# Attention inside a three-part transformer kernel: matmul steps regrouped in threes, and the rotary multiply by the sine moved ahead of the pair swap

## What is computed

```
x = x + 0.5 * ffn(layernorm(x))
x = x + attn(layernorm(x))
x = x + 0.5 * ffn(layernorm(x))

attn(x):                                  # 16 heads of 64
    h = layernorm(x) * ln_scale + ln_bias
    c_q, c_kv = h @ w_down_q.T, h @ w_down_kv.T           # 256 -> 128
    q, k, v = c_q @ w_up_q.T, c_kv @ w_up_k.T, c_kv @ w_up_v.T
    q, k = rope(q), rope(k)      # rot = (e*cos - o*sin, e*sin + o*cos), e and o the even and odd dims
    out = softmax(q @ k.T / 8) @ v
    return out @ w_out.T + x
```

## Time and profile before

| | before |
|---|---|
| time, median of 3 runs | 4203.93 us (4203.29 to 4210.23) |
| time of the profiled execution | 4204.82 us |
| its span, first to last instruction | 4202.9 us |
| PE busy, share of the span | 3943.4 us, 94% |
| DVE, ACT, POOL busy | 2964.9, 2769.4, 3018.6 us (71%, 66%, 72%) |
| mean granted TensorE clock | 0.986 |

### The profile page before, as it was taken

One profiled execution on the slowest core, in us unless ns is written; L12 is line 12 of the kernel. 1 busy time (PEld: TensorE's weight loads), 2 busy tenths in 40 slices (PEclk: granted clock), 3 DMA queues, 4 the chain that ended last, 5 costly groups with the idle time before them and its releaser, 6 DMA issues. The chain is left out here.

```text
span 4202.9 us, 66226 instructions
## 1 busy us (share of the span) xinstructions
PE 3943.4 (94%) x24908; PEld 2235.9 (53%) x24908; DVE 2964.9 (71%) x3709; ACT 2769.4 (66%) x3532; POOL 3018.6 (72%) x1634
## 2 busy tenths in 40 slices
PE   7999979999999999999999999999999999989999
PEld 6888834444444444444444444444444444468888
DVE  5656568777777776877777777777777877555563
ACT  4444457777777777777777777777776777744544
POOL 3444458888888887888788788888887888734443
PEclk9999989999999999999999999999999999999999
DMA  3333221112211211121122112111211121133331
GB/s 110 106 121 112 73 91 54 57 54 67 71 52 52 79 54 52 60 78 51 52 65 69 53 56 81 52 51 59 74 55 57 58 72 62 42 110 105 121 111 61
DMA packets 192775, 300.39 MB, mean 71 GB/s; under 512 B 50327, under 2 KB 100936, under 8 KB 191816
## 3 DMA queue, kind: packets, MB, share of 16 engines
q1 hardware_dynamic: 192456, 296.17, 21.9%
HBM read 201.20 MB, written 26.73 MB: 54 GB/s over the span
## 5 line engine op out<-in xcount | busy, mean ns | idle before, releaser
L1072 DVE TENSOR_REDUCE atNM<-atPS 128x2 f32<-128x1024 f32 x1024 | 1208.0, 1220 | 568.5 <-PE atPS L873 563.0
L1170 POOL TENSOR_TENSOR atACC<-atACC,atPT 128x1024 f32<-128x1024 f32 x510 | 1277.2, 2504 | 69.0 <-ACT atPT L1010 15.0
L1010 ACT ACTIVATE atPT<-atPS 128x1024 f32<-128x1024 f32 x1024 | 995.3, 1022 | 197.3 <-PE atPS L894 187.3
L905 PE MATMUL atPO<-atPT,atV 128*64 128x512 f32 x4096 | 972.5, 595 | 0.0
L1001 ACT ACTIVATE atPS<-atSH 128x1024 f32<-128x1024 f32 x768 | 767.5, 1023 | 39.7 <-DMA atSH<-atMD 24.9
L1170 POOL TENSOR_TENSOR atACC<-atPT 128x1024 f32<-128x1024 f32 x255 | 624.7, 2450 | 105.7 <-PE atOT L927 102.8
L873 PE MATMUL atPS<-atKH,atQH 64*128 64x512 f32 x2048 | 456.5, 448 | 124.0 <-ACT atPT L1010 112.3
L1149 POOL TENSOR_TENSOR atVT<-atVT,atSIN 128x512 f32<-128x512 f32 x254 | 331.0, 1303 | 295.9 <-DMA atVT<-atR 295.9
L905 PEld LDWEIGHTS atPO<-atPT,atV 128*64 128x64 f32 x4096 | 281.6, 137 | 472.9 <-issue 466.6
L894 PE MATMUL atPS<-atQH,atKL 64*128 64x512 f32 x2048 | 469.0, 454 | 38.0 <-ACT atPS L1001 35.2
L894 PE MATMUL atPS<-atQH,atKH 64*128 64x512 f32 x2048 | 405.3, 391 | 0.0
(11 more groups left out here) (280 smaller groups left out, 6835.9 us busy)
## 6 DMA issues: line engine op xcount, KB each, us to landing
atSH<-atMD SPq DMA_DIRECT2D x128, 512.0 KB, 4.5
atVT<-atR SPq DMA_DIRECT2D x508, 128.0 KB, 2.1
f1GB<-f1GD SPq DMA_DIRECT2D x128, 256.0 KB, 7.2
f2GB<-f2GD SPq DMA_DIRECT2D x128, 256.0 KB, 6.9
atRSUM<-atRD SPq DMA_DIRECT2D x126, 256.0 KB, 4.0
X<-x SPq DMA_DIRECT2D x4, 1024.0 KB, 6.0
XS<-x SPq DMA_DIRECT2D x16, 256.0 KB, 3.9
x<-X SPq DMA_DIRECT2D x16, 256.0 KB, 2.7
```

Source lines behind the costliest of these rows:

```text
L905: ins = pe.eng.matmul(PO[HI[h], :], V[n % 2][:, j, HI[h]], PT[k % NPT][:, h, :], start=j == 0, stop=j == T - 1)
L1010: act.eng.activation(PT[k % NPT][:, :, :], PS[ring.of[step]][:, :, :], ACT.Exp, scale=SCALE).then_inc(grown.sem)
L1072: dve.eng.tensor_reduce(NM[:, q // 4, :, q % 4, t], PS[ring.of[step]][:, :, :], AX.X, ALU.max, negate=True).then_inc(most_out.sem)
L1170: pool.eng.tensor_tensor(total[:, :, :], begun[:, :, :], PT[k % NPT][:, :, :], ALU.add).then_inc(gathered.sem)
```

## The change

- The tables' keys become ticks, one for each tile, 16 a unit (`begin` and `early` the even ticks, `late` and `end` the odd).
- The order is written three tiles at a time (`x`, `x + 1`, `x + 2`), as two groups of three uses of the ring: score, most, score, and then most, score, most. One fill stands between the two exponentials of the first group. The attend of tile `x - 1` and the others of tick `x` follow the first group, the attends of `x` and `x + 1` and the others of `x + 1` and `x + 2` the second.
- `sine` and its multiply on POOL go, and ACT's copy of the piece to `R`. DVE multiplies the piece by the sine into `R` straight from `OT`, ahead of the swap, and by the cosine as before. `rotate` moves from DVE to POOL, and subtracts where it added, since the swap now turns the sign.
- `high` of k moves one tick ahead, `high` of q to where that of k stood, `shift` one tick ahead. `NAT` goes from 3 to 4.

```diff
-    NAT = 3
+    NAT = 4
...
-            begin, early, late, end = {}, {}, {}, {}
+            begin, early, late, end = ((0, 0), {}), ((0, 1), {}), ((1, 0), {}), ((1, 1), {})
...
-                table.setdefault(PER * (m - 1) + period, []).extend(steps)
+                (tick, _), steps_of = table
+                steps_of.setdefault(2 * (PER * (m - 1) + period) + tick, []).extend(steps)
...
                     at(early, m, k - 6, ("raise", m, i, t))
-                    at(end, m, k - 5, ("sine", m, i, t))
-                    at(late, m, k - 4, ("rotate", m, i, t))
-                at(early, m, 0, ("high", m, 1))
-                at(end, m, 0, ("high", m, 0), ("klow", m))
+                    at(end, m, k - 5, ("rotate", m, i, t))
+                at(end, m, -1, ("high", m, 1))
+                at(early, m, 0, ("high", m, 0))
+                at(end, m, 0, ("klow", m))
...
-                    at(end, m, 6 + 4 * t, ("shift", m, t))
+                    at(early, m, 6 + 4 * t, ("shift", m, t))
...
+            for x in range(-42, 2 * PER * (NN + 4), 3):
+                order += tile("score", x) + most_of(x) + tile("fill", x + 2) + tile("score", x + 1)
+                order += others_of(x) + tile("attend", x - 1)
+                order += [step for step in tile("gather", x - 1) if step[3] % 4 and step[1:3] + (step[3] // 4,) != (NN - 1, 1, 1)]
+                order += most_of(x + 1) + tile("score", x + 2) + most_of(x + 2)
+                if x % T == T - 1:
+                    order += tile("fill", x + 3) + tile("attend", x) + others_of(x + 1) + tile("fill", x + 4) + tile("attend", x + 1)
+                else:
+                    order += tile("fill", x + 3) + others_of(x + 1) + tile("fill", x + 4) + tile("attend", x) + tile("attend", x + 1)
+                order += [step for i in range(2) for step in tile("gather", x + i)
+                          if step[3] % 4 and step[1:3] + (step[3] // 4,) != (NN - 1, 1, 1)] + others_of(x + 2)
...
@@ scalar
-                    elif name == "raise":
...
-                        act.eng.activation(R[k][:, :], place(step), ACT.Copy).then_inc(raw.sem)
@@ vector, raise
-                        dve.wait_ge(*raw(n, i, t))
+                        dve.wait_ge(*raised(n, i, t))
...
+                        dve.eng.tensor_tensor(R[k][:, :], place(step), SIN[:, sl], ALU.mult).then_inc(raw.sem)
...
-                    elif name == "rotate":
...
-                        dve.eng.tensor_tensor(U[:, i, sl], U[:, i, sl], VT[k][:, :], ALU.add).then_inc(rotated.sem)
@@ gpsimd
-                    elif name == "sine":
+                    elif name == "rotate":
...
-                        pool.eng.tensor_tensor(VT[k][:, :], VT[k][:, :], SIN[:, t * 512:(t + 1) * 512], ALU.mult).then_inc(sined.sem)
+                        pool.wait_ge(*cosine(n, i, t))
+                        pool.eng.tensor_tensor(U[:, i, sl], U[:, i, sl], VT[k][:, :], ALU.subtract).then_inc(rotated.sem)
```

38 lines of the change are left out of this document (14 added, 24 removed).

## The result

| | before | after |
|---|---|---|
| time, median of 4 runs each on one chip | 4206.96 us (4203.29 to 4210.23) | 4152.01 us (4144.14 to 4158.46) |
| ratio, 95% interval | | 0.9869 (0.9849 to 0.9889) |
| profiled execution | 4204.82 us | 4144.14 us |

The change saves 55 us, 1.3%. The sign is the forecast's and the time lies in its range of 3980 to 4200, but the gain is less than half of the 116 us forecast, and the time is 2 us above the 4030 to 4150 that the forecast gave its own chance of 0.61: it falls at the edge of rival 2's stretch. The profiled execution of the changed kernel is the fastest of its four, so the two traces differ by 61 us where the medians differ by 55.

A forecast was written before the change was run, and what follows sets the result against it. PE, busy 94% of the span, was taken as the bound. -184 + 68 = -116 us, with 144 us of new waits and 118 of old taken as equal: 4204.8 - 116 = 4089 us. Range 3980 to 4200; 4030 to 4150 at 0.61.

The forecast's parts named there:

- rival 2: POOL becomes attention's bound, its waits staying whole: 47.8 us a unit, about 4169 us; chance 0.10 (4150 to 4213).
- The wait of the second most: On PE, the second most waits 0.36 us for an exponential in each of 512 periods; threes remove it: 184 us saved.
- The crossings: On PE, 171 more ways there and back between 64-row and 128-row steps, at 0.4 us each: 68 us added.
- The new waits: New order's stalls: empty middle slot 45, raise in second slot 43, end of head's half 30, shift 26; together 144 us.
- the old ones: Score weight loads' 241 waits for ACT's fill before the change, less 0.23 us hidden each: 118 us, replaced by the new order.
- The rotation at 0: Rotation moved among POOL, DVE and ACT: 178 us less DVE work, but none is the bound, so 0 from the path.
- the bound of 25 us: DMAs and queues, SP's hold of swaps included: priced at 0, at most one engine crossing, 0.1 us x 254.
- The shift: Its row stands 8 us ahead of its fill; ACT 0.6 us over in 43 of 128 halves: 26 us, bounds 0 and 205.
- Rival 1: PE nears its own bound, new waits hiding behind each other and old fill waits gone: 3971 us; chance 0.19 (3940 to 4030).
- Rival 3: Fill between two exponentials, late DVE: PE stalls 0.7 us in each of 341 triples, 239 us, 4328 us; chance 0.10 (above 4213).
- Rival 4: The 0.59 us between two mosts is a property of mosts, no wait for the ring; given no chance of its own.
- The signs: Expected in trace: most's waits below 100 us, unit 46.5 us, maxima 1.22 us, score waits for fills below 174, `atSH` 25 to 100.

The follow-up runs named there:

- split_mosts: The kernel before with one line changed: early steps (a raise or a value) put between the two mosts; 4163.48 us.
- extra_crossing: The changed kernel with the attend of the tile before moved between the first score and first most of each triple; 4482.46 us.
- rotate_dve_four: The changed kernel with the rotation's subtract on DVE, at the tick of the old add, and four buffers VT instead of two; 4200.08 us.
- threes_alone_four: The new order in threes with the rotation of before, and four buffers VT instead of two; 4327.1 us.
- both_light: The changed kernel with each maximum over half the keys and each fill over half the columns (work left out); 4009.13 us.
- pool_light: The changed kernel with POOL's rotation and division over only 128 of each 512 columns (work left out); 4151.37 us.
- fill_behind: The changed kernel with the fill between the two exponentials of a triple put behind both; 4146.14 us.
- middle_fill_dve: The changed kernel with DVE making the middle fill of each triple, 341 fills instead of 256; 4140.29 us.
- middle_shift: middle_fill_dve with the shift's read put right behind its write on SP, one tick earlier; 4144.39 us.
- most_first: The changed kernel with each triple's first group as most, score, score: 4145.18 us; a second version with DVE's fills reassigned to match: 4144.76 us.
- no_branch: The changed kernel without the branch where a head's half ends, so a fill stands ahead of the attends there too; 4182.2 us.
- threes_alone: The new order in threes with the rotation of before (ACT's copy, sine on POOL, add on DVE); 4376.56 us.
- rotation_alone: The order of before with the new rotation (sine multiply on DVE, subtract on POOL, no ACT copy); 4254.61 us.

## Why the prediction was half right

**The wait of the second most, -184: right.** PE's delays there were 188 us, the mosts never stand side by side, and split_mosts saves 42 us by this alone, net of some 155 us of crossings.

**The crossings, +68: right in kind, a little too dear.** 0.35 us each by the rows of after and of extra_crossing, where 0.4 was taken; that is 60 us for 171. With all delays under 0.15 us the rise is 43 us. Part of the difference: the first 128-row step followed a second most after 0.43 us and follows a score or a lone most after 0.32, so the 0.20 read at that place was half a crossing and half the late start of the second most. The late starts that went with the wait gave back some 30 us; the forecast had taken their 0.10 us for a part of the crossings' price. The condition "wrong if the crossings cost more than 0.4" was not met.

**The new waits, 144, against the old ones, 118: the step that failed.** The text said "Against them stand the old waits for fills, 118 us, which this order replaces ... I take these two as equal." The new side came out about as sized. With the 62 us of delays that were no waits for fills before (12 at attends, 50 into `OT`) it makes 206, and PE's delays after are 197. Its split was off: scores and mosts 98, attends 39, `OT` 60. The old side was the error. It was taken from 241 waits of the weight load, 174.1 us, less 0.23 us each. PE itself stood idle for those fills far less, as another row of the same view of before shows:

```profile
PE atPS L894 <- ACT atPS L1001: 35.2, 47, 4.9
```

The same row of the changed kernel has 35.2 us too, in 77 times, so this row shows the size of the error but not the change; the starts show both.

On PE's starts all delays of scores and mosts before, other than the second most's, are 51 us. Of the 174.1 us, 128.7 (128 waits) passed beside attends, whose pairs run for 0.43 us and more, and 36.1 (109 waits) beside scores. With 51 in the place of 118 the same sum gives -184 + 68 + 144 - 51 = -23, and with the 43 measured for crossings and small delays in the place of 68, -48; the units measured -57.5. That the two remaining errors are small is in part luck: the new side's parts were off by up to 30 us each, with both signs. The starts would have shown this ahead of time, as they did for the most.

**The rotation at 0: wrong as a part, and not seen as a partner.** Alone it costs 47 us and the order in threes alone 168 (up to 58 of it by the clock); only together do they gain. Two terms hid in the zero. The two multiplies hold `OT` (the forecast had them, at 43 us, but only for the raise in the second slot; in the order of before they cost 49). And SP: "SP, which holds a swap until the one before is rotated, is held for less. I price it at 0." That wait is gone in after, and rotate_dve_four and threes_alone_four put 70 and 50 us on that, up to 22 and 36 of them by way of the clock, of a kind that the bound of 25 us did not hold (no row was given for its 0.1 us). It was no gain over the kernel before, whose shift had 9.3 us; in the order of threes it is what keeps the shift ahead of its fill.

**The shift, 26: small, as forecast.** ACT waits 32.7 us for `atSH`, inside the 25 to 100 named. One tick later it would have cost 40 more, so the change's own move of `shift` carries weight.

**The rivals.** Rival 1 (3971) would need nearly all of the 197 us gone; even both_light, with half the work in maxima and fills, stays at 4009. Rival 2, POOL as the bound, gave a time (4169) near the measured one for a wrong reason: its waits for the swap fell from 295.9 to 70.8 us instead of staying whole, those that are left are beside the path, and pool_light gains nothing. That also answers the sign of POOL's gathers holding the exponentials. Rival 3's mechanism is there, in part: the score that wants the middle fill and the last most of the second group start late in a quarter to a third of the triples (101 and 79 of 325), not in each, for 80 us and not 239. extra_crossing shows what it costs when there is no room for it. Rival 4 falls with the 0.23 us beside each most.

**The signs.** The most's waits for an exponential are 157.1 us and not below 100. A unit takes 47.43 us and not 46.5. The maxima stayed at 1.22 us. Waits of scores for ACT's fills are 106.0 us, below 174 as expected, and yet PE's delays of scores and mosts (98) are more than before (51): 132 of the 164 waits (73.1 us) now stand behind a most, a step of 0.23 us.

**Open.** fill_behind, middle_fill_dve, middle_shift and the two most_first all end within 12 us of after, while half the maxima or half the fills give 76 and 72 us: among these five orders it is the work in the chain that sets the delays, not its order (no_branch and extra_crossing show that other orders cost); which of the remaining 109 us in both_light could go was not tried. The 127 us between threes_alone_four and rotate_dve_four are argued from one wait, not shown. What the clock cost in each run is bounded, not measured.

## What to carry to other kernels

A wait of a weight load costs its engine only what shows between the starts of matmuls. Size a wait that you remove and a wait that you credit by the same view, the starts, or the sum compares a cost with a number that was mostly hidden. A late start costs its wait and a little more, and a wait of some us can be followed by steps at the lower clock, so look at the clock before a loss is put down to waits alone. And a part that costs nothing by its engine's busy share can be the condition of another: look at what an in-order queue holds behind the wait that the part shortens (here a swap that waited on SP, and behind it the shift), and don't add up parts that share such a queue.

## What the hardware showed beyond the forecast

- A 64-row pair that started late cost 0.10 us more than its wait: the next 128-row step came 0.43 us after it, where one follows a score or most on time after 0.32 (2004.66 to 2004.98, 2008.03 to 2008.35). The same 0.43 stands behind the 413 mosts of split_mosts that follow a 128-row step. In the kernel before, 24 second mosts on time also had it, which the late start doesn't explain.
- Long waits of PE were followed by stretches at half the granted clock: after 5.66 us idle in threes_alone and 2.69 us in no_branch, pairs stood 0.43 us apart instead of 0.23, and the clock of the stretch was 0.51 in no_branch.
- Changing between 64 and 128 rows cost 0.35 us there and back in the changed kernel and in extra_crossing (granted clocks of 0.986 and 0.979 over the run): 0.10 going in, 0.15 on the last 128-row step, 0.10 on the first pair of 64 rows.
- The gathers on POOL got faster without being touched. The earlier trace rows had 2504 ns for L1170:

```profile
L1177 POOL TENSOR_TENSOR atACC<-atACC,atPT 128x1024 f32<-128x1024 f32 x510 | 1243.7, 2439 | 85.6 <-ACT atPT L1019 35.5
```

They took 2425 ns in rotation_alone and 2499 in threes_alone, where the add of two SBUF inputs was still on DVE. That is the direction in which the Trainium skill (SBUF — State Buffer, section Who interferes with whom) has it, and it was worth nothing here. The lower part of Q (`atQL`) on DVE went from 2602 to 2150 ns, but it took 2147 in threes_alone and 2493 in rotation_alone: so there most of the fall goes with the order in threes and not with the rotation; what POOL does beside it was not taken apart.
